# First stage of a Mamba and mixture-of-experts kernel: token tiles loaded once into a ring of four, gates made earlier, the low-rank projection one step sooner, and another order in the last steps

## The reference, cut to what matters

```python
# z = layernorm(x), shape (4, 1024, 1024); hidden_states = ctx, shape (4, 1024, 512)
x = jnp.einsum('ed,bld->bel', in_proj_w, hidden_states)
xc = causal depthwise convolution of x over 4 positions
u = jax.nn.silu(xc + conv_b[None, :, None])
x_dbl = jnp.einsum('ke,bel->bkl', x_proj_w, u)            # 64 rows: 32 dt, 16 B, 16 C
delta = jax.nn.softplus(jnp.einsum('er,brl->bel', dt_proj_w, dt_lo) + dt_proj_b[None, :, None])
state = state * exp(delta * A) + (delta * u)[..., None] * B_t     # the scan
y = (y + D[None, :, None] * u) * jax.nn.silu(z)
```

## Time and profile before

| | |
|---|---|
| median of 3 runs | 4338.12 us (4333.21 to 4339.75) |
| the profiled execution, device time | 4337.49 us |
| its span, first to last instruction | 4335.7 us |
| outside the span | 1.8 us |
| first stage in the span | 0 to 595.4 us |
| last `in_proj` ends, the drain starts | 444.5 us |
| TensorE busy over the whole span | 3890.1 us (90%) |
| mean granted TensorE clock | 0.957 of full |

### The profile page before, as it was taken

One profiled execution on the slowest core, in us unless ns is written; L12 is line 12 of the kernel. 1 busy time (PEld: TensorE's weight loads), 2 busy tenths in 40 slices (PEclk: granted clock), 3 DMA queues, 4 the chain that ended last, 5 costly groups with the idle time before them and its releaser, 6 DMA issues. The chain is left out here.

```text
span 4335.7 us, 59481 instructions
## 1 busy us (share of the span) xinstructions
PE 3890.1 (90%) x21088; PEld 3146.4 (73%) x21088; DVE 3011.1 (69%) x3570; ACT 2136.2 (49%) x2201; POOL 1830.9 (42%) x1020
## 2 busy tenths in 40 slices
PE   7887438989889888859999979999999999899999
PEld 3343238878878878848888868888888888688887
DVE  5666549999999999967777745555555555355545
ACT  1666549889988989922222224444444444300000
POOL 0244449999999999933323320000000000022221
PEclk9998659999999999979999989999999999999999
DMA  8676563373373363355455447666666666487543
GB/s 264 221 267 240 200 226 117 113 208 106 110 205 112 113 200 111 104 173 190 169 185 188 169 169 246 232 233 231 232 232 232 232 232 233 172 294 256 198 160 121
DMA packets 331893, 834.51 MB, mean 192 GB/s; under 512 B 66576, under 2 KB 108816, under 8 KB 322512
## 3 DMA queue, kind: packets, MB, share of 16 engines
q1 hardware_dynamic: 299696, 765.01, 52.1%
q0 software_dynamic: 31744, 67.23, 5.2%
q10 hardware_dynamic: 288, 0.07, 0.0%
HBM read 620.42 MB, written 245.27 MB: 200 GB/s over the span
## 5 line engine op out<-in xcount | busy, mean ns | idle before, releaser
L911 POOL TENSOR_TENSOR h<-h,c 128x1024 f32<-128x1024 f32 x512 | 1205.6, 2412 | 54.2 <-DVE h L894 51.4
L894 DVE TENSOR_TENSOR_SCAN h<-da,dbu 128x1024 f32<-128x1024 f32 x512 | 1134.8, 2273 | 74.0 <-ACT dbu L860 52.2
L928 PE MATMUL psb<-m,du_taps 128*128 128x128 f32 x4096 | 580.3, 289 | 133.7 <-ACT dbu L860 84.0
L928 PEld LDWEIGHTS psb<-m,du_taps 128*128 128x128 f32 x4096 | 509.6, 195 | 203.0 <-ACT dbu L860 113.0
L867 ACT ACTIVATE da<-dl,ad 128x1024 f32<-128x1024 f32 x512 | 588.9, 1150 | 78.8 <-DVE h L894 66.4
L938 PE MATMUL psy<-ident,h 128*128 128x128 f32 x4096 | 561.0, 281 | 43.4 <-POOL h L911 25.2
L860 ACT ACTIVATE dbu<-psb 128x1024 f32<-128x1024 f32 x512 | 523.3, 1022 | 84.8 <-PE psb L928 74.1
L1647 POOL DMA_INDIRECT xg<-scratch_xn,ids x64 | 63.4, 990 | 1056.0 <-PE psT L1667 1032.4
L1807 DVE TENSOR_TENSOR wsp<-raw,wsp 128x2048 fp32r<-128x2048 f32 x192 | 434.1, 2289 | 105.6 <-ACT wsp L1760 105.6
L938 PEld LDWEIGHTS psy<-ident,h 128*128 128x128 f32 x4096 | 446.9, 143 | 76.4 <-POOL h L911 50.1
L1760 ACT ACTIVATE wsp<-raw 128x2048 fp32r<-128x2048 f32 x192 | 359.2, 1909 | 19.4 <-DMA raw<-in_w 19.3
(11 more groups left out here) (191 smaller groups left out, 7576.5 us busy)
## 6 DMA issues: line engine op xcount, KB each, us to landing
raw<-in_w SPq DMA_DIRECT2D x192, 1024.0 KB, 6.8
du_taps<-scratch_duT SPq DMA_DIRECT2D x512, 128.0 KB, 2.9
scratch_duT<-duT SPq DMA_DIRECT2D x64, 512.0 KB, 3.1
c<-scratch_c SPq DMA_DIRECT2D x64, 512.0 KB, 8.8
scratch_xT<-xT_s SPq DMA_DIRECT2D x32, 1024.0 KB, 4.9
scratch_ob<-ob SPq DMA_DIRECT2D x64, 512.0 KB, 2.7
xT_s<-scratch_xT SPq DMA_DIRECT2D x32, 1024.0 KB, 5.1
xs<-in_x SPq DMA_DIRECT2D x32, 512.0 KB, 5.3
```

What stands on the lines that cost most here:

```text
L894: dve.tensor_tensor_scan(h[:, k % HR, :], da[k % 2][:, :], dbu[:, (k // GN) % 2, k % GN, :], 0.0, ALU.mult, ALU.add).then_inc(s_scan, 1)
L911: pool.tensor_tensor(h[:, k % HR, :], h[:, k % HR, :], c[:, n, :], ALU.mult).then_inc(s_hc, 1)
L928: mm = pe.matmul(psb[:, j], duT[:, r * CP + j, :], m[:, g // 2, :, r * CP + j, g % 2 * GN:(g % 2 + 1) * GN], start=True, stop=True)
```

## The change

1. **One load.** `xs` goes. A token tile is loaded once into `xz`, now a ring of four (`ZR`); statistics and gate both read it there. `gate_copy` writes the transposed gate back into the tile's own place in the ring, `szT` goes, and `store_gate` stores from there. A load waits for the store of the tile four before it.
2. **Gates early.** Roots are made for two tiles (`ZG` 2), so 16 times and not 8. A table `z_steps` sets the steps: tiles 0 to 15 are counted in steps 1 to 11 and gated in steps 2 to 12 (two a step in 2, 3, 5, 6, 8, 9, 11, 12), tiles 16 to 31 are gated one a step in 15 to 18, 20 to 23, 25 to 28 and 30 to 33.
3. **Low rank a step sooner.** `XP` 1, `DT` 9, `LOG` 11, `DUT` 13; the loop has 46 steps. `low_rank` is first in ScalarE's step and `xd_rest` second in VectorE's.
4. **B.** `b_head` first copies the transposes to `bF`, and `psV` is free after that one copy. `store_b` is spread over four steps, `clear_b` over the four batches. `convolve` is last in VectorE's step, `b_rest` a step later.
5. **The drain.** From step 32 the queues have another order; GpSimd only makes log1p, VectorE adds delta (`delta_sum`) and multiplies; the relu is back on ScalarE, and `dt_proj` only uses `psV`.

```diff
-        Q, SR, ZG = B * ET, 4, 4
-        USILU, XP, ZS, SZT, DT, LOG, DUT = 1, 2, ZG, ZG + 1, ET + 2, ET + 4, ET + 6
+        Q, SR, ZG, ZR = B * ET, 4, 2, 4
+        USILU, XP, DT, LOG, DUT = 1, 1, ET + 1, ET + 3, ET + 5
+        def z_steps(g):
+            if g < ET:
+                a = 1 + 3 * (g // 2) + g % 2
+                return (a, a), (a + 1, a + 1)
+            a = 13 + (g - ET) * 5 // 2
+            return (a, a + 1), (a + 2, a + 3)
...
+            def load_x(k):
+                after(sp, s_szst[k % ZR], (k // ZR) * 16)
+                sp.dma_start(xz[:, k % ZR, :], x_tile(k)).then_inc(s_xz[k % ZR], 16)
...
+            def gate_copy(k):
+                act.wait_ge(s_sztr, k + 1)
+                act.activation(xz[:, k % ZR, :], psV[:, :], ACT.Copy).then_inc(s_szev, 1)
...
             def b_head(b):
                 act.wait_ge(s_bttr, b + 1)
+                after(act, s_btlo, b)
+                act.activation(bF[:], vT[:, :, 0:NST], ACT.Copy).then_inc(s_bf, 1)
+                act.wait_ge(s_bf, b + 1)
...
+            def delta_sum(q):
+                e = q % SR
+                dve.wait_ge(s_lc, q + 1)
+                dve.tensor_tensor(rbuf[:, e, :], rbuf[:, e, :], lbuf[:, e, :], ALU.add).then_inc(s_dl, 1)
+                times_u(dve, q)
...
             def step(s):
-                on_tile(s, DUT, du_rest)
-                on_tile(s, 0, gate_stats)
-                if s % ZG == ZG - 1 and s < Q:
-                    gate_scales(s // ZG)
...
+                b = batch_at(s, 1)
                 if b is not None:
                     xd_rest(b)
...
+                if drain(s):
+                    on_tile(s, LOG + 1, lambda q: delta_sum(q) if tail(q) else None)
+                on_tile(s, LOG, correction)
+                if drain(s):
+                    on_tile(s, DUT, du_rest)
+                for k in z_counted[s]:
+                    gate_stats(k)
+                    if k % ZG == ZG - 1:
+                        gate_scales(k // ZG)
+                on_tile(s, 0, convolve)
```

More of the change, by code:

```diff
@@ L252, in mamba_inputs @@
         tail = lambda q: q >= Q - LOG
-        late = lambda q: q >= Q - ET
+        drain = lambda s: s >= Q
         def du_bank(q):
-            bank = psX[q % 2] if q + DUT >= Q else psV
+            bank = psX[q % 2] if drain(q + DUT) else psV
             return bank[:].rearrange("p (t c) -> p t c", c=P)
[L259 to L264, removed]
         @block.sync
@@ L306, in store_c, with store_b @@
                 sp.dma_start(dr["c"][b], xd[DR + NST:DR + 2 * NST, :]).then_inc(s_cst, 16)
[L308 to L321, removed]
+            def store_b(b, part, twin):
+                if part == 0 and twin == 0:
+                    sp.wait_ge(s_bthi, b + 1)
+                    sp.wait_ge(s_btlo, b + 1)
+                    sp.wait_ge(s_btz, 16 * (b + 1))
+                for k in range(P // TB):
+                    band = dr["bT"][b, part]
+                    diagonal = bass.AP(band.tensor, band.offset + twin * BAND * ROW + k * ET * NH,
+                                       [[SKEW, TB], [TB * SKEW, 2], [1, ET * NH]])
+                    sp.dma_start(diagonal, f32(bT[k::P // TB, part]).rearrange("t h j n -> t h (j n)")).then_inc(s_btst, 16)
             def store_delta(q):
@@ L375, in _, with take_v @@
             pe.wait_ge(s_first, 32)
+            readers = []
+            def take_v(*then):
+                for sem_, n in readers:
+                    pe.wait_ge(sem_, n)
+                readers[:] = then
             def in_proj(q, hb):
@@ L401, in dt_proj @@
                     pe.wait_ge(s_wdlo, 2)
[L402 to L411 removed]
+                take_v((s_abs, q + 1))
                 for hb in range(2):
[L413 removed]
+                    mm = pe.matmul(psV[:, hb * HB:(hb + 1) * HB], w_dts[:, et * P:(et + 1) * P],
                                    xds[:, hb * HB:(hb + 1) * HB], start=True, stop=True)
```

234 lines of the change are left out of this document (112 added, 122 removed).

## The result

| | before | changed |
|---|---|---|
| median of 4 runs each | 4335.66 us (4332.69 to 4339.75) | 4307.25 us (4305.96 to 4307.87) |
| span of the profiled execution | 4335.7 us | 4306.1 us |

The ratio is 0.9926, with a 95% interval of 0.9914 to 0.9939: faster, by 28 us at the median and 29.6 us in the span. The forecast was 4260 and its range ended at 4292; the time lies 47 us above the one and 15 us above the other.

What follows compares the result with a forecast made beforehand. The prediction took TensorE, with its pauses and lower clock behind them, to bound the first stage, and a three-engine loop its drain. Terms 11 + 30 + 37 = 78 us off 4337.5 gave 4260 (range 4230 to 4292).

Steps and rivals of the forecast that it cites:

- term 1: First stage up to the in-projection of step 17: 25 us of pauses gone, 14 against, net 11 (0 to 22).
- term 2: First stage, steps 17 to 31, two batches: 39 us gained, 6 and 3 against, net 30 (12 to 45).
- the gates' 9.62 and their slow stretch: Up to step 17: TensorE's 9.62 us pause for a token tile behind zeros, plus lower-clock time after it; 12 us gone.
- the low-rank hand-over: Once a batch, dt projection waits for VectorE's subtractions: pause of 8.6 + 2.3 us falls to 4 and 1, gain 6.
- Term 3: The drain, from the end of the last in-projection: last transposes end at 104.9 and not 141.5; net 37 (25 to 47).
- The step of the loop: Drain: correction on VectorE, log1p on GpSimd, sum and product on VectorE; 7.0 us a step, seven steps.
- Rival 1: First stage: VectorE is the bound, 8 more chains of 3.2 us = 26; 4279, or 4285; chance 0.19.
- its sign in the trace: For VectorE as the bound: pauses of TensorE that end with a convolution or a rest in most steps.
- Rival 2: First stage: nearly all pauses go, also low-rank and odd-step waits; 110 us off, 4228; chance 0.16.
- Rival 3: Drain: one PSUM tile for dt, ScalarE pays the dt projection's 1.19 in 8 steps: 10 us, 4270; chance 0.05.
- Rival 4: Ring of four: loads wait for gate stores, 8.4 us for each of 14 pairs; 40 us slower, 4378; chance 0.03.
- Rival 5: Low rank a step sooner does nothing, VectorE's convolution holds the hand-over; 4 x 6 less gain, 4284; chance 0.05.

Runs made afterwards that it cites:

- roots_first: Changed kernel with statistics and roots moved ahead of the correction in VectorE's step, nothing else; 4256.32 us, ratio 0.9815; second set of runs 4259.46 us, 0.9817.
- roots_first_lag2: roots_first with the low-rank work back a step later (XP 2, DT 10, LOG 12, DUT 14); 4260.59 us, ratio 0.9824.
- first_fused: roots_first with each Newton turn in three instructions and not four, nothing left out; 4244.56 us, ratio 0.9783.
- before_roots_late: Kernel before the change with only `gate_scales` moved behind the correction on VectorE; 4374.65 us, ratio 1.0085.

## Why the prediction was wrong

| us | to the in-projection of step 17 | to the end of the last in-projection | to the end of the last transposes |
|---|---|---|---|
| before | 221.7 | 222.8 | 141.5 |
| forecast | 210.7 | 192.8 | 104.9 |
| changed | 222.8 | 222.4 | 111.2 |
| roots_first | 213.3 | 191.9 | 104.6 |

**The step that failed** is the price of a chain of roots: "five more at 324.47 - 321.28 = 3.2 us, 16 us on VectorE, which in the ramp has room: 2" in term 1, and in term 2 "seven chains of roots and not four, and each now sits directly ahead of a convolution. One chain cost 2.01 us at 332.81; three more, 6". Of the nine chains that stand behind a correction eight take 8.0 us and one 6.7. I took the duration from a row in which GpSimd was idle, and used it for a place in which GpSimd runs, since the correction just ahead is what releases it. The prediction looked at what stood behind the chain, the convolution, and not at what the instruction ahead of it sets going on another engine. It also had the like of this in hand: GpSimd's 3.21 beside VectorE's product and 2.35 beside its reads of PSUM. It used that for GpSimd and never asked for VectorE.

With the chain at its old price, and the rest of the change as it is, the terms come out close to the forecast (roots_first):

- **Term 1**, forecast 11, brought 8.4. In the changed kernel it is -1.1: the gates' 9.62 and their slow stretch did go, but the wait for the rest at 200.53 is 7.23 and not 2.78 as in roots_first, each with its slow stretch, and a gate's transposes wait 5.2 us for ScalarE's output of the dt projection, where roots_first has at most 1.8. The first dt projection's wait, the low-rank hand-over of the first batch, is 5.4 in both, where the prediction left 4.
- **Term 2**, forecast 30, brought 30.9. In the changed kernel it is 0.4.
- **Term 3**, forecast 37, brought 36.9. The first dt projection of the last batch starts 23.2 us behind the last in-projection (428.41 - 405.2), forecast 23.3; in the changed kernel 29.7 (474.93 - 445.2), because a held chain in the last step put the last convolution's end at 12.0, where it is 6.8 in roots_first and 7.3 in the forecast. The step of the loop is 6.87 us in both, forecast 7.0:

```profile
545.01 1.23 DVE L653 TENSOR_TENSOR rbuf<-rbuf,lbuf 128x1024 f32<-128x1024 f32 x1 [1.39 <-POOL lbuf L705]
546.27 1.23 DVE L256 TENSOR_TENSOR ebuf<-rbuf,u 128x1024 f32<-128x1024 f32 x1
547.41 0.68 DVE L641 TENSOR_SCALAR cbuf<-ebuf 128x1024 f32<-128x1024 f32 x1
...
551.87 1.23 DVE L653 TENSOR_TENSOR rbuf<-rbuf,lbuf 128x1024 f32<-128x1024 f32 x1 [1.39 <-POOL lbuf L705]
```

These rows of the changed kernel answer to the earlier trace rows. GpSimd's log1p sum takes 2.34 us there, as taken from the earlier trace rows, and the time to the scan's first transfer is 10.8 us (567.15 - 556.4), forecast 9.4.

Inside terms 1 and 2 the gain of the low-rank hand-over came, but not from the step sooner. In roots_first its three pauses ahead of the drain are 5.4, 3.2 and 4.2 us, in roots_first_lag2, without the step sooner, 3.2, 5.2 and 3.0; before they were 7.5, 8.6 and 8.6, and the forecast left 4. TensorE's and ScalarE's time lines, first before, then roots_first, then roots_first_lag2:

```profile
230.00 1.93 PE L424 MATMUL psD<-u,w_x 128*64 128x512 f32 x4
241.82 1.02 ACT L497 ACTIVATE xd<-psD 64x1024 f32<-64x1024 f32 x1
```

```profile
210.00 1.93 PE L422 MATMUL psD<-u,w_x 128*64 128x512 f32 x4
214.11 1.02 ACT L497 ACTIVATE xd<-psD 64x1024 f32<-64x1024 f32 x1
```

```profile
219.23 1.93 PE L422 MATMUL psD<-u,w_x 128*64 128x512 f32 x4
223.35 1.02 ACT L497 ACTIVATE xd<-psD 64x1024 f32<-64x1024 f32 x1
```

ScalarE's copies end 10.9 us behind the projection before and 3.2 us behind it in both others, which have in common that `low_rank` stands first in ScalarE's step. What is left of the pause is VectorE's other work ahead of the subtractions, the convolution and the rest of du. No run moves `low_rank` alone. So the prediction had the gain and this reason for it right, and the lag brought nothing ahead of the drain.

**The rivals.** Rival 1 comes nearest, and its sign in the trace was seen, if in some steps and not in most: pauses of TensorE that end with a rest. But its reason, eight more chains of 3.2 us, is not the main one: with all 16 chains and none held, the time is 4256. It priced 19 us, and the holding cost 48. It holds in part, since shorter chains do gain: 9.6 us less in first_fused brought at least 8.8. Rival 2 did not occur: waits for the low-rank rest of 3 and 4 us stay in roots_first. Rival 3: the drain's step is as forecast, and its sums come every 6.87 to 6.89 us also while dt projections still run, so one tile for dt costs nothing in the loop; no run gives the second tile back. Rival 4: no wait of SyncE's ring ended a pause of TensorE; the first gates waited 0.80 us. Rival 5 was right that the step sooner does nothing ahead of the drain (behind it 3 us by the time lines), and wrong in its price, since the hand-over's pause shrank without it.

## What to carry to other kernels

Before the duration of a small instruction is taken to another place, look in the time line at what GpSimd does at the old place and at the new one: the same 0.17 us cost up to 2.2. In this kernel the chains of tiny SBUF instructions on VectorE were best placed ahead of the instruction that releases GpSimd. Behind GpSimd's work they were short as well, but came too late for those who wait for them. Where a kernel gains less than its terms say, look at the groups of lines for a mean that rose without its shape having changed.

## What the runs showed of the hardware that I had not expected

- A 128x2 `tensor_scalar` or `tensor_tensor` of VectorE on SBUF that starts while a 128x1024 `tensor_tensor` of GpSimd runs ends 0.01 to 0.04 us behind it, in all 26 cases of the changed kernel and all 15 of before_roots_late: 0.93, 2.22 and 2.21 us in the chain shown, and not 0.17. A 128x1024 `tensor_scalar` is held as well (2.84 us and not 0.69, roots_first). One that starts 0.01 to 0.02 us ahead of GpSimd's next passes at 0.16 to 0.17.
- GpSimd is hardly touched by this: its instructions took 2.35 to 2.38 us there and 2.34 to 2.37 in roots_first.
- The holding cost 1.3 us for each us of it in two pairs of kernels (48 for 36 net, 40 for 30.5), in the changed kernel with a granted clock of 0.89 in the second part where roots_first has 0.96, but 0.4 (8 to 9 for 22 net) in a third, without the Newton turns.
